# Weight checks read as 16-bit halves, padding rows copied by DMA, and relative keys transposed on TensorE, in a two-layer attention and feed-forward kernel

## The chip, the cores and the metric

One NeuronCore of a Trainium2 chip runs the whole program in one launch. The metric is the device time of one execution in microseconds (us), the median of several. Times within the kernel count from the start of the profiled span.

## What is computed

The input is x, float32, 4 batches of 1024 tokens of 128 features. There are two halves, each "layernorm, layer, layernorm, add to x". The first layer is causal attention with 16 heads of 8 features and relative keys, the second a gated feed-forward network with ternary weights (-1, 0, 1) and a scale per output.

```python
scores = jnp.einsum('bhid,bhjd->bhij', q, k)
rel = jnp.einsum('bhid,pd->bhip', q, rel_key)          # 256 relative keys
rel_idx = jnp.clip(j - i + p - 1, 0, p - 1)
bias = jnp.take_along_axis(rel, rel_idx, axis=3)
logits = jnp.where(causal, (scores + bias) * scale, -jnp.inf)
attn = jax.nn.softmax(logits, axis=-1)
x = x + _layernorm(attn @ v @ Wo + bo)                 # heads joined
h = silu(xn @ w1.T * s1) * (xn @ w2.T * s2)            # xn = layernorm(x)
h = gelu(h @ h1.T * sh1); h = gelu(h @ h2.T * sh2)
x = x + _layernorm(h @ w3.T * s3)
```

The kernel works on the weights of the feed-forward network in a rounded form, and checks first that this loses nothing: the weights as loaded must have no low bits. The result of this check is one of two flags; a later stage takes another way if a flag is set. With ternary weights it isn't.

## The kernel before, in words

The program has a first stage (lines 319 to 713), a stage that is skipped unless a flag is set (`largest_scores`, line 1291), the attention proper (lines 881 to 1290, here "stage two"), and the feed-forward network (`stage3`, line 1423). Each is a block in which the engines run their own lists of instructions, tied by semaphores, and a block begins when all engines have left the one before. The change lies in the first alone.

Stage one goes through the four batches b. VectorE makes the layernorm of the tokens (`layernorm`, lines 444 to 470: `stats`, `mv`, `var_e`, then `std` from ScalarE's `root`, line 570, then eight instructions that write `xh`). TensorE transposes `xh` (line 663), ScalarE copies the result to `xT` (line 579), TensorE projects q, k and v (lines 673 and 681) into the PSUM tensors `p_q`, `p_k`, `p_v`. ScalarE adds the biases (`qf`, `kf`, lines 609 and 611), and ScalarE and VectorE split q and k into three bfloat16 parts each (`q_parts`, `k_parts`). GpSimd writes a copy of q in another order, `q_turned` (line 435). From k's largest and smallest value (`k_ext`, line 495) and q TensorE computes a bound on each row's scores in `p_tr` (lines 691 to 693), the "shift"; ScalarE and VectorE split it into three parts too (`m_neg`, `m_rest`, `m_parts`, lines 633, 638, 480, 584 and 484), the last two of them one batch later (`shift_rest`, `shift_mid`, `shift_low`). Batch b + 1's layernorm and projections are issued in batch b, ahead of its own bound. For the second and third of its four batches the body is a loop of the sequencers.

SyncE issues every DMA of the stage, in one order: tokens of batch 0 into `x_all` (line 324); eight parameter loads, all counted by one semaphore `s_par` (line 333), the last two being `bv_b` (one row of 512 B written eight times into each of 128 partitions) and `rel_t`, the 256 relative keys of 8 features with features as rows, so that each element of 4 B is a piece of its own; tokens of batch 1; the relative keys' parts to DRAM and back (lines 338 to 345, from `rel_p` and `gx`, which VectorE computes in lines 535 to 546); tokens of batches 2 and 3, each when the ones before have landed; the feed-forward weights into `every`, 5632 columns in 128 partitions (line 353). Then per batch the shift of the batch before (line 359) and nine stores of the parts of q, k and turned q (lines 376 to 382), each when it is made. In the last batch the loads for stage two go ahead of these (lines 369 to 372), when all stores of batch 2 have landed.

TensorE, VectorE and ScalarE each wait for all eight parameters, `s_par` at 8 * 16, before the first projection, before the work on the relative keys, and before the first `qf`. VectorE then also waits for `g_ext`, which comes back from DRAM, before its batch 0 (line 547).

The tensors `q_sb` and `k_sb` of stage two have 96 rows. Loads fill 75 and 72 of them; the rest must be 0 in `q_sb` and 1 in `k_sb`. GpSimd writes them at the start by memsets of rows 64 to 95, 4096 columns each (lines 424 and 425).

The check of the weights has three parts. For each, ScalarE writes `every` rounded to `low_part` (`rounded`, line 591), GpSimd subtracts it (`remainder`, line 404), and ScalarE takes the absolute value with the sum along the row (`largest`, line 596). Parts 0 and 1 are rounded at the end of batch 0; the rest of ScalarE's work stands at the head of the last batch and after it. VectorE joins the sums (lines 553 and 555) before `shift_rest(B - 1)`, line 556.

Of the kernel before, what the change touches and what calls it, by code (L numbers as in the profile page):

```python
# [24 lines left out]
P = 256  # L25
# [123 lines left out]
def build(nc, ctx, x, Wq, bq, Wk, bk, Wv, bv, Wo, bo, rel, w1, s1, w2, s2, h1, sh1, h2, sh2, w3, s3, out):  # L149
# [59 lines left out]
    rel_t = sb("rel_t", [HD, P], F32, one)  # L209
# [27 lines left out]
    low_part = [sb(f"low_part{i}", [128, (HC * E * 2 + HC * HID * 2 + HID) // CHECKS + 1], F32R, one) for i in range(2)]  # L237
# [6 lines left out]
    s_par = sem("s_par")  # L244
    s_gs = sem("s_gs")
# [30 lines left out]
    s_whi, s_wlo, s_wabs, s_wany, s_wsum = (sem(n) for n in ("s_whi", "s_wlo", "s_wabs", "s_wany", "s_wsum"))  # L276
# [42 lines left out]
    with nc.Block() as block:  # L319
        @block.sync  # L320
        def _(sp):
# [5 lines left out]
            for dst, src in ((wq_sb[:, :], Wq), (wk_sb[:, :], Wk), (wv_sb[:, :], Wv),  # L327
                             (bq_c[:, :], bq.rearrange("(p a) -> p a", a=1)),
                             (bk_c[:, :], bk.rearrange("(p a) -> p a", a=1)),
                             (r0_c[:, :], ap(rel.tensor, 0, [[0, H], [1, HD], [1, 1]])),  # L330
                             (bv_b[:, :, :], ap(bv.tensor, 0, [[0, 128], [0, NB], [1, 128]])),
                             (rel_t[:, :], ap(rel.tensor, 0, [[1, HD], [HD, P]]))):
                sp.dma_start(dst, src).then_inc(s_par, 16)
# [13 lines left out]
            for b in range(2, B):  # L347
                sp.wait_ge(s_xin, b * 16)
                tokens(b)
            sp.wait_ge(s_rw, 32)  # L350
# [10 lines left out]
            def batch(b, first, last):  # L361
                if last:

                    sp.wait_ge(s_pool, 16)
                    sp.wait_ge(s_qst, 16 * PARTS * b)
                    sp.wait_ge(s_kst, 16 * PARTS * b)
                    sp.wait_ge(s_mst, 16 * (b - 1))
                    sp.wait_ge(s_rst, 16 * PARTS * b)
                    sp.dma_start(q_rows[:, :], ap(qr_dram, 0, [[DROW, PARTS * HD], [0, PARTS], [1, UH * S]])).then_inc(t_qr[0], 16)
                    load_k(0, 0)  # L370
                    load_q(0, 0)
# [19 lines left out]
        def checked(i):  # L391

            n = every.shape[1] // CHECKS + 1
            c = slice(i * n, min((i + 1) * n, every.shape[1]))
            return every[:, c], low_part[i % 2][:, 0:c.stop - c.start]

        @block.gpsimd
        def _(pool):

            def remainder(i):  # L400

                pool.wait_ge(s_whi, i + 1)
                got, part = checked(i)
                nc.gpsimd.tensor_tensor(part, got, part.bitcast(F32), ALU.subtract).then_inc(s_wlo, 1)
# [17 lines left out]

            for p in range(2):
                step(nc.gpsimd.memset(q_sb[p][64:KROWS, :], 0.0), 9 + 4 * p)
                step(nc.gpsimd.memset(k_sb[p][64:KROWS, :], 1.0), 10 + 4 * p)
                pad = v_sb[p][:, :, :].rearrange("p n (h d) -> p n h d", h=HG)
                step(nc.gpsimd.memset(pad[:, :, :, HD:32], 0.0), 11 + 4 * p)
                step(nc.gpsimd.memset(pad[:, :, :, HD:HD + 1], 1.0), 12 + 4 * p)

            for b in range(B):  # L430
# [6 lines left out]
                if b == 0:  # L437
                    remainder(0)
                    remainder(1)
            remainder(2)  # L440

        @block.vector
        def _(dve):
# [42 lines left out]
            def batch(b, first, last_batch):  # L486
# [10 lines left out]
                dve.wait_ge(s_kx, b * KX + 2)  # L497
                nc.vector.tensor_tensor(k_ext[:, :], k_ext[:, :], g_ext[:, 0:2], ALU.add).then_inc(s_kx, 1)
# [33 lines left out]
            dve.wait_ge(s_par, 8 * 16)  # L532
            nc.vector.tensor_tensor(kb_c[:, :], bk_c[:, :], r0_c[:, :], ALU.add).then_inc(s_gs, 1)

            nc.vector.tensor_scalar(rel_s[:, :], rel_t[:, :], rel_t[:, 0:1], None, ALU.subtract).then_inc(s_gs, 1)
# [11 lines left out]
            dve.wait_ge(s_gld, 16)  # L547
# [21 lines left out]
        def _(act):  # L569
# [16 lines left out]
            def rounded(i):  # L586
                act.wait_ge(s_every, 16 * len(WEIGHTS))
                if i >= 2:
                    act.wait_ge(s_wabs, i - 1)
                got, part = checked(i)  # L590
                nc.scalar.activation(part, got, ACT.Copy).then_inc(s_whi, 1)

            def largest(i):
                act.wait_ge(s_wlo, i + 1)
                _, part = checked(i)
                nc.scalar.activation(part, part.bitcast(F32), ACT.Abs, accum_out=low_max[:, i:i + 1]).then_inc(s_wabs, 1)

            def batch(b, first, last_batch):
                if last_batch:
                    largest(0)  # L600
                    rounded(2)
                    largest(1)
                if not last_batch:
# [7 lines left out]
                nc.scalar.activation(kf[:, :], p_k[:, :], ACT.Identity, bias=kb_c[:, 0:1]).then_inc(s_kf, 1)  # L611
                if not last_batch:
# [26 lines left out]
                if first:  # L639
                    rounded(0)  # L640
                    rounded(1)
# [3 lines left out]
            act.wait_ge(s_par, 8 * 16)  # L645
            act.wait_ge(s_gs, 1)
            batches(act, batch)
            largest(2)
# [3 lines left out]
        def _(pe):  # L652
# [49 lines left out]

            transposes(0, True)
            pe.wait_ge(s_par, 8 * 16)
            project_qk(0, True)
            project_v(0, True)
            pe.wait_ge(s_gs, 10)
# [1204 lines left out]
```

## Time and profile before

| | |
|---|---|
| median of 3 runs | 788.54 us (788.49 to 788.73) |
| profiled execution | 789.45 us, span 787.7 us |
| TensorE busy | 646.7 us, 82% of the span |
| VectorE, ScalarE busy | 565.0 us (72%), 562.4 us (71%) |
| GpSimd busy | 301.0 us (38%) |
| DMA | 52.79 MB in 41169 packets, mean 67 GB/s |
| largest line of the chain that ended last | TensorE, lines 1653 and 1656 (`stage3`), 7% each |

Engine times are sums of spans in which the engine had an instruction in work. In the timeline a row gives start, length, engine, line, operation, output and inputs, the number of instructions merged, and in brackets the idle time before it and what ended that. "SPq" is SyncE issuing a DMA; its length is the time of issue, not of the transfer, and a wait inside merged issues is in it. In the rows by windows, DMA share is the mean busy share of 16 DMA engines and PEclk the TensorE clock that was granted, 1.00 being 2.4 GHz and 0.50 being 1.2 GHz.

### The profile page before, as it was taken

The numbers are of one execution on the slowest core, as the hardware profiler recorded it, in microseconds if no ns is written. First come the engines' busy times: TensorE is split into PE (matmuls) and PEld (weight loads), VectorE is DVE, ScalarE is ACT, GpSimd is POOL, SyncE is SP. The second block draws the span as 40 slices with busy tenths as digits, with TensorE's granted clock in tenths as the row PEclk, the third lists the DMA queues.
The fourth block names the chain that finished last, engine by engine and source line by source line (L and its number), as shares of the span: only waits on it lengthen the run. The fifth ranks groups of instructions, "written<-read, shape, count | busy, mean of one in ns | idle before, by whom it ended". The sixth has DMA issues, their size and how long they took to land. (4 is left out here: it accounts for less than half of the span.)

```text
span 787.7 us, 19097 instructions
## 1 busy us (share of the span) xinstructions
PE 646.7 (82%) x8064; PEld 470.4 (60%) x8064; DVE 565.0 (72%) x927; ACT 562.4 (71%) x657; POOL 301.0 (38%) x190
## 2 busy tenths in 40 slices
PE   0667632679999999999999999987779899898993
PEld 0323310556767667676676766855568678687682
DVE  7589963367877778777787777876665757768546
ACT  0264572369898898988988879887757867778563
POOL 9074233813608136081360722701053181451801
PEclk9986866579999999999999999998989999999998
DMA  3470375311422314223152231514020000000001
GB/s 64 103 247 8 117 200 177 70 31 37 121 62 63 94 36 122 62 64 94 32 125 62 64 93 32 125 30 135 14 81 2 0 1 1 0 28 1 0 28 55
DMA packets 41169, 52.79 MB, mean 67 GB/s; under 512 B 7410, under 2 KB 31554, under 8 KB 38658
## 3 DMA queue, kind: packets, MB, share of 16 engines
q1 hardware_dynamic: 41082, 51.54, 24.3%
q8 instruction: 65, 1.06, 0.6%
q14 instruction: 22, 0.18, 0.1%
HBM read 39.59 MB, written 11.94 MB: 65 GB/s over the span
## 5 line engine op out<-in xcount | busy, mean ns | idle before, releaser
L960 PE MATMUL p_s<-q_sb,k_sb 96*128 96x128 bf16 (+1 forms) x1600 | 170.8, 249 | 18.7 <-DVE probs L1106 14.9
L1224 ACT ACTIVATE probs<-p_s 128x1024 f32<-128x1024 f32 x160 | 156.8, 1018 | 17.8 <-DVE p_s L1115 10.8
L1224 ACT ACTIVATE probs<-probs 128x1024 f32<-128x1024 f32 x128 | 133.7, 1057 | 46.4 <-DVE probs L1106 46.2
L1004 PE MATMUL p_o<-probs,v_sb 128*32 128x128 f32 (+1 forms) x3200 | 159.1, 330 | 7.6 <-ACT o_acc L1242 5.3
L960 PEld LDWEIGHTS p_s<-q_sb,k_sb 96*128 96x128 bf16 x1600 | 112.7, 100 | 77.7 <-issue 29.0
L916 POOL TENSOR_SCALAR_AFFINE_SELECT even_b<-even_b 128x2048 f32<-128x2048 f32 x32 | 75.5, 2360 | 216.3 <-ACT even_b L1235 216.3
L1106 DVE TENSOR_TENSOR probs<-p_s,even_b 128x1024 f32<-128x1024 f32 x96 | 115.0, 1220 | 28.4 <-PE p_s L960 16.0
L1004 PEld LDWEIGHTS p_o<-probs,v_sb 128*32 128x32 f32 x3200 | 84.5, 111 | 40.7 <-issue 13.5
L1653 PE MATMUL p_z<-hid_hi,h_hi 128*128 128x512 f32 x256 | 102.3, 399 | 1.7 <-POOL hid_lo L1574 1.7
L1656 PE MATMUL p_z<-hid_lo,h_hi 128*128 128x512 f32 x256 | 100.8, 394 | 0.0
L981 PE MATMUL p_s<-q_rows,rel_w 72*128 72x64 bf16 x2048 | 84.8, 197 | 18.2 <-DVE probs L1106 8.7
L981 PEld LDWEIGHTS p_s<-q_rows,rel_w 72*128 72x128 bf16 x2048 | 76.9, 101 | 28.1 <-DVE probs L1106 10.7
L1858 DVE TENSOR_TENSOR hid_lo<-act_f,hid_hi 128x512 fp32r<-128x512 f32 x64 | 55.6, 882 | 41.7 <-ACT hid_hi L1756 41.7
L920 POOL TENSOR_SCALAR_AFFINE_SELECT even_b<-even_b 128x2048 f32<-128x2048 f32 x32 | 75.5, 2359 | 7.5 <-POOL even_b L916 7.5
L1127 DVE COPY even_b<-p_s 128x1024 f32<-128x1024 f32 x40 | 48.8, 1221 | 27.7 <-PE p_s L981 27.5
L1755 ACT ACTIVATE act_f<-p_z,sh_c 128x512 f32<-128x512 f32 x64 | 44.4, 694 | 28.5 <-PE p_z L1656 28.4
L1653 PEld LDWEIGHTS p_z<-hid_hi,h_hi 128*128 128x128 f32 x256 | 48.2, 188 | 13.8 <-POOL hid_lo L1574 2.6
L1656 PEld LDWEIGHTS p_z<-hid_lo,h_hi 128*128 128x128 f32 x256 | 48.2, 188 | 10.6
L435 POOL COPY q_turned<-q_parts 128x1024 bf16<-128x1024 bf16 x12 | 30.9, 2581 | 61.8 <-ACT q_parts L620 43.4
L1127 DVE COPY odd_b<-p_s 128x896 f32<-128x896 f32 x32 | 34.8, 1087 | 23.7 <-PE p_s L981 23.7
L1106 DVE TENSOR_TENSOR probs<-p_s,odd_b 128x1024 f32<-128x1024 f32 x32 | 39.1, 1223 | 13.9 <-PE p_s L960 13.9
L1756 ACT ACTIVATE hid_hi<-p_z,sh_c 128x512 fp32r<-128x512 f32 x64 | 44.1, 689 | 0.0
(176 smaller groups left out, 925.0 us busy)
## 6 DMA issues: line engine op xcount, KB each, us to landing
k_sb<-k_dram SPq DMA_DIRECT2D x48, 192.0 KB
q_sb<-q_dram SPq DMA_DIRECT2D x16, 576.0 KB
q_rows<-qr_dram SPq DMA_DIRECT2D x42, 192.0 KB
q_dram<-q_parts SPq DMA_DIRECT2D x12, 256.0 KB, 3.5
k_dram<-k_parts SPq DMA_DIRECT2D x12, 256.0 KB, 3.8
qr_dram<-q_turned SPq DMA_DIRECT2D x12, 256.0 KB, 3.5
x_all<-in_L_attn_x_dram SPq DMA_DIRECT2D x4, 512.0 KB, 4.1
every<-in_L_ffn_h_w_dram SPq DMA_DIRECT2D x2, 1024.0 KB, 8.3
```

The source lines that it names most:

```text
L916: nc.gpsimd.affine_select(out=far, in_=near, compare_op=ALU.is_ge, fill=0.0, base=-1 - r, pattern=[[0, QB], [-1, MCH * RCH]], channel_mult ...
L920: nc.gpsimd.affine_select(out=near, in_=near, compare_op=ALU.is_ge, fill=MASKED, base=r, pattern=[[0, QB], [1, MCH * RCH]], channel_multip ...
L960: last = nc.tensor.matmul(slot[:, c:c + n * BLK], k_sb[hg][:, h * S + j * BLK:h * S + (j + 1) * BLK], ap(q_sb[hg], at, [[HG * S, KROWS], [ ...
L981: last = nc.tensor.matmul(slot[:, x * QB:(x + 1) * QB], rel_w[0:ROWS, w0:w0 + BLK], q[:, r, :, :], start=True, stop=True)
L1004: last = nc.tensor.matmul(p_o[32 * h:32 * h + 32, at:at + blocks * BLK], v_sb[hg][:, j, h * 32:(h + 1) * 32], probs[n % PBUFS][:, h, col * ...
L1106: last = nc.vector.tensor_tensor(probs[m % PBUFS][:, hp * 2:hp * 2 + 2, :], columns(slot, 0, run), term, ALU.add)
L1127: nc.vector.tensor_copy(to, got).then_inc(t_cd, 1)
L1224: nc.scalar.activation(to, got, ACT.Exp, scale=SCALE).then_inc(t_exp, 1)
L1653: nc.tensor.matmul(to[:, :], whi[w][:, j, cols], hi[j], start=(j == 0), stop=False)
L1656: last = nc.tensor.matmul(to[:, :], whi[w][:, j, cols], lo[j], start=False, stop=(j == len(hi) - 1))
L1755: nc.scalar.activation(act_f[k][:, o, :], bank(tile)[:, :], ACT.Gelu, scale=sc).then_inc(f_act, 1)
L1858: nc.vector.tensor_tensor(hid_lo[k][l % 2][:, o, :], act_f[k][:, o, :], hid_hi[k][l % 2][:, o, :].bitcast(F32), ALU.subtract).then_inc(f_l ...
```

## The change

The check of the weights becomes three ScalarE passes, of 2048, 2048 and 1536 columns, at the end of batch 0. Each reads the lower 16 bits of every float as an unsigned number, every other 16-bit number of `every`, and sums them along the row. Nothing of it is left in the last batch, and GpSimd has no part in it. The rows of padding come from a small tile `pads` (two memsets of 512 columns) by four DMAs, issued behind the tokens of batch 3 and waited for on SyncE before `every` is loaded. The relative keys are loaded as they lie, 128 keys in as many partitions, 32 B a piece, first of the parameters, and transposed by two TensorE instructions into `p_v`. VectorE reads them there, with one column copied to `gx` first. The semaphore of the parameters is split: `s_relt` for the keys, `s_wts` for the three weights, `s_par` for the last four. `kb_c` moves behind the work on the relative keys, the wait for `g_ext` moves into batch 0, and in batch 0 ScalarE's `root(1)` moves behind `kf`.

```diff
-    rel_t = sb("rel_t", [HD, P], F32, one)
+    rel_n = sb("rel_n", [128, P // 128, HD], F32, one)
+    pads = sb("pads", [128, 2, 512], BF16, one)
...
-    low_part = [sb(f"low_part{i}", [128, (HC * E * 2 + HC * HID * 2 + HID) // CHECKS + 1], F32R, one) for i in range(2)]
+    low_part = sb("low_part", [128, HC * HID], F32, one)
...
             tokens(0)
-            for dst, src in ((wq_sb[:, :], Wq), (wk_sb[:, :], Wk), (wv_sb[:, :], Wv),
-                             (bq_c[:, :], bq.rearrange("(p a) -> p a", a=1)),
+            sp.dma_start(rel_n[:, :, :], ap(rel.tensor, 0, [[HD, 128], [128 * HD, P // 128], [1, HD]])).then_inc(s_relt, 16)
+            for dst, src in ((wq_sb[:, :], Wq), (wk_sb[:, :], Wk), (wv_sb[:, :], Wv)):
+                sp.dma_start(dst, src).then_inc(s_wts, 16)
+            for dst, src in ((bq_c[:, :], bq.rearrange("(p a) -> p a", a=1)),
...
-                             (bv_b[:, :, :], ap(bv.tensor, 0, [[0, 128], [0, NB], [1, 128]])),
-                             (rel_t[:, :], ap(rel.tensor, 0, [[1, HD], [HD, P]]))):
+                             (bv_b[:, :, :], ap(bv.tensor, 0, [[0, 128], [0, NB], [1, 128]]))):
                 sp.dma_start(dst, src).then_inc(s_par, 16)
...
             for b in range(2, B):
                 sp.wait_ge(s_xin, b * 16)
                 tokens(b)
+            sp.wait_ge(s_pool, 9)
+            for p in range(2):
+                for rows, dst, which in ((ROWS + PARTS, q_sb[p], 0), (ROWS, k_sb[p], 1)):
+                    n = KROWS - rows
+                    sp.dma_start(ap(dst, rows * (HG * S), [[HG * S, n], [512, HG * S // 512], [1, 512]]),
+                                 ap(pads, which * 512, [[2 * 512, n], [0, HG * S // 512], [1, 512]])).then_inc(s_pads, 16)
+            sp.wait_ge(s_pads, 16 * 4)
             sp.wait_ge(s_rw, 32)
...
                 if last:
-                    sp.wait_ge(s_pool, 16)
...
+            nc.gpsimd.memset(pads[:, 0, :], 0.0)
+            step(nc.gpsimd.memset(pads[:, 1, :], 1.0), 9)
             for p in range(2):
-                step(nc.gpsimd.memset(q_sb[p][64:KROWS, :], 0.0), 9 + 4 * p)
-                step(nc.gpsimd.memset(k_sb[p][64:KROWS, :], 1.0), 10 + 4 * p)
...
-                if b == 0:
-                    remainder(0)
-                    remainder(1)
-            remainder(2)
...
+                if first:
+                    dve.wait_ge(s_gld, 16)
                 nc.vector.tensor_tensor(k_ext[:, :], k_ext[:, :], g_ext[:, 0:2], ALU.add).then_inc(s_kx, 1)
...
             layernorm(0, True)
-            dve.wait_ge(s_par, 8 * 16)
-            nc.vector.tensor_tensor(kb_c[:, :], bk_c[:, :], r0_c[:, :], ALU.add).then_inc(s_gs, 1)
-            nc.vector.tensor_scalar(rel_s[:, :], rel_t[:, :], rel_t[:, 0:1], None, ALU.subtract).then_inc(s_gs, 1)
+            rel_t = p_v[0:HD, 0:P]
+            dve.wait_ge(s_gtr, 1)
+            nc.vector.tensor_copy(gx[:, 2:3], rel_t[:, 0:1]).then_inc(s_gs, 1)
+            dve.wait_ge(s_gs, 1)
+            nc.vector.tensor_scalar(rel_s[:, :], rel_t, gx[:, 2:3], None, ALU.subtract).then_inc(s_gs, 1)
...
-            dve.wait_ge(s_gld, 16)
+            dve.wait_ge(s_par, 4 * 16)
+            nc.vector.tensor_tensor(kb_c[:, :], bk_c[:, :], r0_c[:, :], ALU.add).then_inc(s_gs, 1)
...
-            def rounded(i):
+            def low_bits(i):
                 act.wait_ge(s_every, 16 * len(WEIGHTS))
-                if i >= 2:
-                    act.wait_ge(s_wabs, i - 1)
-                got, part = checked(i)
-                nc.scalar.activation(part, got, ACT.Copy).then_inc(s_whi, 1)
-            def largest(i):
-                act.wait_ge(s_wlo, i + 1)
-                _, part = checked(i)
-                nc.scalar.activation(part, part.bitcast(F32), ACT.Abs, accum_out=low_max[:, i:i + 1]).then_inc(s_wabs, 1)
+                if i > 0:
+                    act.wait_ge(s_wabs, i)
+                n = every.shape[1]
+                c = slice(i * (HC * HID), min((i + 1) * (HC * HID), n))
+                low = every[:, c].bitcast(mybir.dt.uint16).rearrange("p (c two) -> p c two", two=2)[:, :, 0]
+                nc.scalar.activation(low_part[:, 0:c.stop - c.start], low, ACT.Copy,
+                                     accum_out=low_max[:, i:i + 1]).then_inc(s_wabs, 1)
             def batch(b, first, last_batch):
-                if last_batch:
-                    largest(0)
-                    rounded(2)
-                    largest(1)
-                if not last_batch:
+                if not first and not last_batch:
                     root(b + 1)
...
                 nc.scalar.activation(kf[:, :], p_k[:, :], ACT.Identity, bias=kb_c[:, 0:1]).then_inc(s_kf, 1)
+                if first:
+                    root(1)
...
                 if first:
-                    rounded(0)
-                    rounded(1)
+                    for i in range(CHECKS):
+                        low_bits(i)
             root(0)
             transposed(0, True)
-            act.wait_ge(s_par, 8 * 16)
-            act.wait_ge(s_gs, 1)
+            act.wait_ge(s_par, 4 * 16)
+            act.wait_ge(s_gs, 10)
             batches(act, batch)
-            largest(2)
             shift_mid(B - 1)
...
+            pe.wait_ge(s_relt, 16)
+            for x in range(P // 128):
+                last = nc.tensor.transpose(p_v[0:HD, x * 128:(x + 1) * 128], rel_n[:, x, :], ident[:, :])
+            last.then_inc(s_gtr, 1)
             transposes(0, True)
-            pe.wait_ge(s_par, 8 * 16)
+            pe.wait_ge(s_wts, 3 * 16)
             project_qk(0, True)
+            pe.wait_ge(s_gs, 2)
             project_v(0, True)
-            pe.wait_ge(s_gs, 10)
+            pe.wait_ge(s_gs, 11)
             batches(pe, batch)
```

## Rows read from the trace of the kernel before

**Rows 1.** Windows, stage one: busy time (instructions) by engine, PEclk, DMA share, GB/s

```profile
0.00:137.30 137.30, 64.50 (x180) 30.33 (x180) 100.32 (x183) 57.89 (x66) 60.49 (x35) 0.81 0.47 131
```

**Rows 2.** Timeline, 11 to 19 us, VectorE and GpSimd: start, length, engine, line

```profile
11.09 8.65 DVE L468 TENSOR_SCALAR xh<-x_all,rstd,nmr 128x128 f32<-128x128 f32 x8
...
14.99 3.54 POOL L425 MEMSET k_sb<- 32x4096 bf16 x1
```

**Rows 3.** DMA packets of 8 to 18 and of 18 to 22 us, tokens' issue and landing

```profile
DMA packets 882, 0.39 MB, mean 39 GB/s; under 512 B 116, under 2 KB 882, under 8 KB 882
...
DMA packets 2364, 0.22 MB, mean 54 GB/s; under 512 B 1956, under 2 KB 2364, under 8 KB 2364
...
5.74 14.11 SPq L323 DMA_DIRECT2D x_all<-in_L_attn_x_dram  x1
...
DMA to landing us min/median/max: 4.1/4.1/19.9
```

**Rows 4.** SyncE's issues 26 to 39 us, landing of the weights, window 38 to 48 us

```profile
26.96 0.31 SPq L338 DMA_DIRECT2D g_dram<-rel_p  x1
...
30.82 4.51 SPq L323 DMA_DIRECT2D x_all<-in_L_attn_x_dram  x2
35.37 1.44 SPq L353 DMA_DIRECT2D every<-in_L_ffn_w_w_dram  x2
...
38.15 0.78 SPq L353 DMA_DIRECT2D every<-in_L_ffn_w_w_dram  x1
...
DMA to landing us min/median/max: 4.3/7.4/9.7
...
38.00:48.00 10.00, 9.31 (x20) 3.94 (x19) 9.90 (x12) 6.09 (x7) 7.04 (x2) 0.69 1.04 354
```

**Rows 5.** Timeline, 24 to 38 us, VectorE and ScalarE

```profile
24.28 0.16 DVE L533 TENSOR_TENSOR kb_c<-bk_c,r_c 128x1 f32<-128x1 f32 x1 [4.54 <-DMA rel_t<-in_L_attn_rel_key_dram]
...
31.52 1.64 DVE L449 BATCH_NORM_STATS2 stats<-x_all 128x6 f32<-128x128 f32 x8
...
34.27 0.21 ACT L572 ACTIVATE std<-var_e 128x8 f32<-128x8 f32 x1 [11.80 <-DVE var_e L456]
...
34.96 2.23 DVE L468 TENSOR_SCALAR xh<-x_all,rstd,nmr 128x128 f32<-128x128 f32 x8
...
37.10 1.22 DVE L495 TENSOR_REDUCE k_ext<-kf 128x1 f32<-128x1024 f32 x1
```

**Rows 6.** Timeline, 52 to 64 us, ScalarE, GpSimd and VectorE

```profile
52.61 3.41 ACT L591 ACTIVATE low_part<-every 128x1878 fp32r<-128x1878 f32 x2
54.45 7.61 POOL L404 TENSOR_TENSOR low_part<-every,low_part 128x1878 fp32r<-128x1878 f32 x2 [3.08 <-ACT low_part L591]
55.92 0.19 ACT L572 ACTIVATE std<-var_e 128x8 f32<-128x8 f32 x1
...
58.75 5.18 DVE L468 TENSOR_SCALAR xh<-x_all,rstd,nmr 128x128 f32 x8
```

**Rows 7.** Timeline, 101 to 110 us, ScalarE at the head of the last batch

```profile
101.24 1.76 ACT L596 ACTIVATE low_part<-low_part 128x1878 fp32r<-128x1878 f32 x1
...
108.60 1.05 ACT L620 ACTIVATE q_parts<-qf 128x1024 bf16<-128x1024 f32 x1
```

**Rows 8.** Window 110 to 124 us, landing of the shifts, the end of stage one

```profile
110.00:124.00 14.00, 8.09 (x12) 2.22 (x12) 12.20 (x13) 5.77 (x7) 7.58 (x4) 0.67 0.78 189
...
DMA to landing us min/median/max: 2.2/2.3/6.1
...
125.02 1.06 ACT L638 ACTIVATE m_parts<-m_neg 16x1024 bf16<-16x1024 f32 x1 [2.65 <-DMA m_dram<-m_parts]
127.03 1.77 ACT L596 ACTIVATE low_part<-low_part 128x1876 fp32r<-128x1876 f32 x1 [0.95 <-POOL low_part L404]
...
129.20 1.20 DVE L480 TENSOR_TENSOR m_rest<-m_neg,m_parts 16x1024 f32<-16x1024 f32 x1
```

**Rows 9.** Window 160 to 168 us, where TensorE's work of stage two comes back

```profile
160.00:168.00 8.00, 6.26 (x72) 4.41 (x72) 5.95 (x6) 5.06 (x5) 1.11 (x3) 0.56 0.07 20
```

More of the change, by code:

```diff
@@ L244, in build @@
     s_par = sem("s_par")
+    s_wts = sem("s_wts")
+    s_relt = sem("s_relt")
+    s_pads = sem("s_pads")
+    s_gtr = sem("s_gtr")
     s_gs = sem("s_gs")
@@ L275, in build @@
     s_every = sem("s_every")
-    s_whi, s_wlo, s_wabs, s_wany, s_wsum = (sem(n) for n in ("s_whi", "s_wlo", "s_wabs", "s_wany", "s_wsum"))
+    s_wabs, s_wany = sem("s_wabs"), sem("s_wany")
     s_qst, s_kst, s_mst = sem("s_qst"), sem("s_kst"), sem("s_mst")
@@ L389, in _ @@
             sp.wait_ge(s_mst, 16 * B)
[L391 to L395, printed above, removed]
         @block.gpsimd
         def _(pool):
-            def remainder(i):
-                pool.wait_ge(s_whi, i + 1)
-                got, part = checked(i)
-                nc.gpsimd.tensor_tensor(part, got, part.bitcast(F32), ALU.subtract).then_inc(s_wlo, 1)
             def step(ins, n):
@@ L421, in _ @@
             step(nc.gpsimd.memset(gap_one[:, :], 0.0), 8)
+            nc.gpsimd.memset(pads[:, 0, :], 0.0)
+            step(nc.gpsimd.memset(pads[:, 1, :], 1.0), 9)
             for p in range(2):
-                step(nc.gpsimd.memset(q_sb[p][64:KROWS, :], 0.0), 9 + 4 * p)
-                step(nc.gpsimd.memset(k_sb[p][64:KROWS, :], 1.0), 10 + 4 * p)
                 pad = v_sb[p][:, :, :].rearrange("p n (h d) -> p n h d", h=HG)
-                step(nc.gpsimd.memset(pad[:, :, :, HD:32], 0.0), 11 + 4 * p)
-                step(nc.gpsimd.memset(pad[:, :, :, HD:HD + 1], 1.0), 12 + 4 * p)
+                step(nc.gpsimd.memset(pad[:, :, :, HD:32], 0.0), 10 + 2 * p)
+                step(nc.gpsimd.memset(pad[:, :, :, HD:HD + 1], 1.0), 11 + 2 * p)
             for b in range(B):
@@ L584, in shift_mid @@
                 nc.scalar.activation(m_parts[:, 1, :], m_rest[:, :], ACT.Identity).then_inc(s_mhi, 1)
-            def rounded(i):
+            def low_bits(i):
                 act.wait_ge(s_every, 16 * len(WEIGHTS))
-                if i >= 2:
-                    act.wait_ge(s_wabs, i - 1)
-                got, part = checked(i)
-                nc.scalar.activation(part, got, ACT.Copy).then_inc(s_whi, 1)
-            def largest(i):
-                act.wait_ge(s_wlo, i + 1)
-                _, part = checked(i)
-                nc.scalar.activation(part, part.bitcast(F32), ACT.Abs, accum_out=low_max[:, i:i + 1]).then_inc(s_wabs, 1)
-            def batch(b, first, last_batch):
-                if last_batch:
-                    largest(0)
-                    rounded(2)
-                    largest(1)
-                if not last_batch:
+                if i > 0:
[5 more added lines that the diff above has]
+                                     accum_out=low_max[:, i:i + 1]).then_inc(s_wabs, 1)
+            def batch(b, first, last_batch):
+                if not first and not last_batch:
                     root(b + 1)
```

## The prediction, made before the changed kernel ran

> **What bounds the kernel now.** I read the page first (which engine is busy where), then the windows by stage, then the timeline of the first 137 us with the SyncE queue's own waits, and last the landing times of single tiles. Everything the diff touches lies in stage one. It takes 137.3 us, and no engine fills it: VectorE, the busiest, has 100.3 us, and DMA a share of 0.47 [rows 1]. A chain through several engines bounds it, so each removed piece must be followed to what waits for it next. For the end of the run only one moment counts, the end of stage one: what follows starts from it as before.
>
> At the start, GpSimd's memsets of 32x4096 hold VectorE's normalisation: the eight xh instructions spread over 8.65 us beside memsets of 3.5 us [rows 2], and need 2.23 us with GpSimd idle [rows 5]. But TensorE, VectorE (kb_c) and ScalarE then wait for the parameters until 24.28 us [rows 5], so this is hidden. Of the parameters two are slow. bv_b reads one row of 512 B 1024 times: between 8 and 18 us 882 packets moved only 0.39 MB, 39 GB/s. Only after it come the 2048 four-byte pieces of rel_t: 1956 small packets between 18 and 22 us. The second batch's tokens, issued at 5.74, stand behind both and land after 19.9 us, at 25.7 [rows 3]. The change removes rel_t alone.
>
> **The start of the change.** The relative keys come as 256 pieces of 32 B instead, transposed by two TensorE instructions and read from PSUM; 256 pieces at the small packets' rate of rows 3 (1956 in under 4 us) are 0.5 us, the added copy of one column some 0.15 us, and both finish before xh. Without long memsets xh ends near 10.6; transposes and the q, k projections start by 13.4 instead of 24.3. bv_b stays: its 524 KB at 39 GB/s [rows 3] are 13.4 us, from about 6 to 19.5, and the tokens behind it (512 KB, at the 354 GB/s of rows 4 1.5 us, and near 0.5 to land) arrive near 21.5. That, not the projections, is what VectorE waits for: the second layernorm starts at 21.5 instead of 31.52. With root(1) moved behind kf nothing is late (kf is through by 22, the root is due at 24.2). So k_ext comes at 27.2 instead of 37.10 [rows 5]: **9.9 us earlier**.
>
> **The SyncE queue.** It is here that the change adds a wait. Its stores of the relative keys stand behind the same tokens and land near 21.6; from the store at 26.96 to the third tokens at 30.82 lay 3.9 us, of which about 1.6 were the stores themselves, so 2.3 remain and those tokens go out near 24.0; the fourth need them landed (4.1 us, rows 3) and go at 28.2. Now four new DMAs are issued, 0.6 us each, to about 31, of 21, 24, 21 and 24 rows by 8 KB, 737 KB in all, and the queue waits for them to land, with the five loads of `every` and all stores of batch 0 behind it. Their rate is unknown. The nearest rows are the loads into 72 and 24 rows of the same tiles, 189 GB/s [rows 8]: 3.9 us. The fast end is the 354 GB/s of whole loads [rows 4], 2.1 us; the slow end the 39 GB/s of the other source that is read over and over [rows 3], 19 us. I take 3.9: after the tokens' data at 31.8 the pads land near 36.0. `every` is then first issued at 36.05, where it was 35.37. Before, it ran behind the fourth tokens; the last was issued at 38.15 and landed 9.7 us later, at 47.9. Behind an idle queue 2.88 MB at 354 GB/s are 8.1 us, with the 2.2 that a small transfer takes from issue to landing [rows 8]: **46.4**.
>
> A rule speaks against these DMAs. The Trainium skill, DMA: Bandwidth & Descriptors, section on why a DMA increments its semaphore by 16, says that a transfer uses the largest number of engines up to 16 that divides the slowest dimension of both sides. By it the 21-row transfers run on 7 engines and the 24-row ones on 12. No run here shows the pads yet; the share of 0.78 (12.5 of 16 engines) of rows 8 for 24-row loads agrees. By it the first seven engines carry 80 packets of 1 KB each, with which my 3.9 us would be 49 ns a packet, so the sum would not move much.
>
> **ScalarE.** The two rounding passes of batch 0 started at 52.61, moved to 42.7, and the weights are there at 46.4 to 46.5: 3.8 us of new waiting. Three passes of 2048, 2048 and 1536 columns follow. From 1.05 us for 1024 and 1.76 for 1878 an element costs 0.83 ns [rows 7]: 1.90, 1.90 and 1.48, with 0.18 for the accumulator each, 5.8 to 5.9 in all; two rounding passes cost 3.3 (to the root at 55.92). That the input is every other 16-bit number is not shown: the low end is the same rate, the high end twice it, 4.7 us more; I take the same, since cost per element there went with the count. So the root comes at 52.4 and xh ends 2.9 us behind it (34.27 to 37.19, rows 5), at 55.4. Before, GpSimd's subtractions (from 54.45, 7.6 us) held VectorE: xh began at 58.75 and ended at 63.93 [rows 6]. **8.5 us earlier**, of which 9.9 came in, 3.8 went to the weights, 2.6 to the longer passes, and 5.0 came from GpSimd no longer working beside xh.
>
> **The end of stage one.** Batches 1 and 2 keep their length. In batch 3 the three ScalarE passes from 101.24 are gone, so VectorE's part runs 3 to 5 us sooner (q_parts, at 108.60, only 1, as its buffer waits for batch 2's stores). I count this as hidden: the last m_parts pass, at 125.02, waited 2.65 us for the shift of batch 2, whose store took 6.1 us instead of 2.3, because it stands behind the loads for stage two, which run at a share of 0.78 between 110 and 124 us [rows 8] and start no earlier than before. Behind it largest(2) goes: the final subtraction could begin at 126.1 instead of 129.20: **3.1 us** [rows 8]. GpSimd's last subtraction was beside all this. Were the shift not held, the other stores, moved by the same DMA, would still cap the tail at about 4.6.
>
> Sum: 8.5 + 3.1 = 11.6 us. The profiled execution took 789.45 us (span 787.7), 0.9 over the median of 788.54; 777.9 against it, **776.9** against the median.
>
> **Rivals.**
> 1. The weights come in time, because the pads or bv_b are quicker than thought. Then the passes start at 42.7, the gain at xh is 12.3, with the tail 15.4: 773.1; with the capped tail another 1.5 less, 771.6. For it: nothing has been seen of pads; against: the wait for them is plain, and bv_b's rate is shown. 0.17.
> 2. The strided 16-bit read costs double (gain 6.9, 781.6), or the pads pay bv_b's 13 ns (766 large packets in 10 us, rows 3) for each of 720 packets, 9.4 instead of 3.9 us (gain 6.1, 782.4). For: both forms are new. 0.13.
> 3. **Slower**: the pads go at bv_b's 39 GB/s, since each source row is read 8 times. They take 19 us instead of 3.9, SyncE holds `every` and batch 0's stores 15 us longer, and ScalarE stands before root(2): 15 - 11.6 = 3.4 slower, 792. It turns slower once the pads take over 15.5 us, 48 GB/s. Against: bv_b's rows all came from one place in HBM, these are 90 rows in SBUF. 0.04.
> 4. The start-up gain doesn't show because the tokens, not the layernorm's helpers, were all that mattered: bv_b lasts 4 us longer than I take, with rel_n's pieces among it: gain 7.6, 781. 0.06.
> 5. The clock: TensorE has 0.56 of it between 160 and 168 us when its work comes back [rows 9]. How that falls against work that comes 12 us sooner is open: a few microseconds more or less at half rate, partly hidden behind VectorE; I put 2 us either way on it, within the range.
>
> **The numbers.** My forecast has 0.60, the rivals 0.17, 0.13, 0.04 and 0.06. The range takes in rivals 1, 2 and 4 with the unknown rates: 771.0 to 783.0. Under 0.2% (1.6 us) a measurement of this kernel tells little from no change. Faster 0.93, same 0.03 (pads near 14 us), slower 0.04.
>
> **What the profile after would show.** xh of batch 0 near 8.5 to 10.6, at 2.2 us; stats of the second batch at 21 to 22, behind its tokens; the third tokens at 24, four pad issues at 28 to 31, `every` first issued near 36 (if at 33, rival 1; if beyond 45, rival 3); low_bits behind a wait on `every` at about 46.5, 1.9 us a pass; xh of batch 2 unstretched, ending at 55.4; 3.1 us less between the last m_parts pass and the end of stage one. I am wrong if low_bits starts without a wait, if a pass takes over 2.5 us, if batches 1 and 2 change their length, or if the stages behind differ by more than 2 us.

## The result, and the profile after

The changed kernel takes 783.01 us (781.41 to 783.46, 4 runs) where the kernel before took 788.63 (788.49 to 789.47): ratio 0.9924, interval 0.9910 to 0.9938, so 4.9 to 7.1 us less. The profiled execution took 783.46 us (span 781.7) against 789.45. The forecast was 776.9 in a range of 771.0 to 783.0: the median lies on the upper edge, on the side that was forecast, with half of the gain.

The first 32 us of the changed kernel's timeline, VectorE (start, length, engine, line, operation; in brackets the idle time and what ended it):

```profile
8.38 2.14 DVE L464 TENSOR_SCALAR xh<-x_all,rstd,nmr 128x128 f32<-128x128 f32 x8
...
20.20 0.16 DVE L547 TENSOR_TENSOR kb_c<-bk_c,r_c 128x1 f32<-128x1 f32 x1 [6.88 <-DMA bv_b<-in_L_attn_bv_dram]
...
22.27 1.64 DVE L445 BATCH_NORM_STATS2 stats<-x_all 128x6 f32<-128x128 f32 x8 [1.82 <-DMA x_all<-in_L_attn_x_dram]
...
27.76 1.22 DVE L491 TENSOR_REDUCE k_ext<-kf 128x1 f32<-128x1024 f32 x1
```

Without the long memsets xh takes 2.14 us instead of 8.65 [rows 2]. The wait for `bv_b` ends at 20.20, the second batch's tokens are there at 22.27 (31.52 before) and k_ext comes at 27.76 instead of 37.10 [rows 5]: 9.3 us earlier, where 9.9 were forecast. In the six other runs that keep this start it comes at 28.37 to 28.82, 8.3 to 8.7 us earlier than in the kernel before.

The timeline of SyncE's queue in the same kernel:

```profile
23.95 4.40 SPq L328 DMA_DIRECT2D x_all<-in_L_attn_x_dram  x2
28.40 0.91 SPq L360 DMA_DIRECT2D q_sb<-pads  x1
...
31.05 0.81 SPq L360 DMA_DIRECT2D k_sb<-pads  x1
...
39.36 0.92 SPq L366 DMA_DIRECT2D every<-in_L_ffn_w_w_dram  x2
...
41.43 0.50 SPq L366 DMA_DIRECT2D every<-in_L_ffn_w_w_dram  x1
```

Its windows around the pads, as a whole and in two parts, and around `every` (window, its length, busy time and instructions of PE, PEld, DVE, ACT, POOL, then PEclk, DMA share and GB/s):

```profile
32.00:39.00 7.00, 7.00 (x14) 2.31 (x13) 7.00 (x5) 3.64 (x5) 3.93 (x2) 0.84 0.54 84
...
32.00:34.00 2.00, 2.00 (x3) 0.67 (x2) 2.00 (x2) 1.37 (x2) 1.95 (x1) 0.50 0.76 82
...
36.00:38.00 2.00, 2.00 (x6) 0.74 (x6) 2.00 (x3) 1.19 (x2) 1.81 (x1) 1.00 0.45 105
...
42.00:50.00 8.00, 1.36 (x13) 1.17 (x11) 2.03 (x10) 1.06 (x2) 0.21 (x1) 0.87 0.95 319
```

And the time from issue to landing of `every`'s DMAs in the same kernel, shortest, median and longest:

```profile
DMA to landing us min/median/max: 2.8/7.4/10.2
```

The third tokens go out at 23.95 and the pads at 28.40, as forecast to 0.2 us. Then comes the gap: from 31.9, when the last pad DMA has been issued, SyncE issues nothing for 7.5 us. The pads move at 84 GB/s over a share of 0.54, and `every` goes out at 39.36, 4.0 us later than before the change (35.37, rows 4), in spite of the earlier start. The last of its pieces, issued at 41.43, takes the longest of these times, 10.2 us, to land.

The timeline of ScalarE and VectorE where batch 0 ends, in the same kernel:

```profile
51.69 1.91 ACT L594 ACTIVATE low_part<-every 128x2048 f32<-128x2048 uint16 x1 [8.59 <-DMA every<-in_L_ffn_w_w_dram]
53.50 0.19 ACT L594 ACTIVATION_READ_ACCUMULATOR low_part<-every 128x1 f32 x1
...
57.35 0.19 ACT L572 ACTIVATE std<-var_e 128x8 f32<-128x8 f32 x1
...
58.12 2.14 DVE L464 TENSOR_SCALAR xh<-x_all,rstd,nmr 128x128 f32 x8
```

ScalarE stands 8.59 us for the weights. The passes then take 1.91 us for 2048 columns, 1.90 being what the other ScalarE rows give for as many: reading every other 16-bit number cost nothing more here. The root of batch 2 comes at 57.35, later than the 55.92 of before [rows 6]. What is gained here is all behind it: xh is no longer stretched by GpSimd and ends at 60.26 instead of 63.93, 3.7 us sooner.

The timeline of the last batch and the end of stage one, in the same kernel; the PE row is the first of stage two:

```profile
103.96 1.06 ACT L617 ACTIVATE q_parts<-qf 128x1024 bf16<-128x1024 f32 x1 [4.44 <-DMA k_dram<-k_parts]
...
121.24 1.06 ACT L635 ACTIVATE m_parts<-m_neg 16x1024 bf16<-16x1024 f32 x1 [5.42 <-DMA m_dram<-m_parts]
122.33 1.21 DVE L476 TENSOR_TENSOR m_rest<-m_neg,m_parts 16x1024 f32<-16x1024 f32 x1 [5.49 <-ACT m_parts L635]
...
125.90 0.35 SPq L372 DMA_DIRECT2D m_dram<-m_parts  x1
...
130.52 1.71 PE L982 MATMUL p_s<-q_rows,rel_w 72*128 72x64 bf16 x29 [5.50 <-PEq L1325]
```

The same first row of stage two in the kernel before:

```profile
137.37 1.86 PE L981 MATMUL p_s<-q_rows,rel_w 72*128 72x64 bf16 x32 [5.49 <-PEq L1324]
```

The three passes at the head of the batch are gone, but q_parts waits 4.44 us for the stores of batch 2 and the m_parts pass 5.42 us, not 2.65 [rows 8], for the shift's store. From that pass to m_rest it is 1.1 us instead of 4.2: 3.1 us. Stage two starts 6.85 us earlier (3.7 and 3.1). From there to the end of the execution this profile takes 652.9 us and the one before 652.1, which leaves 6.0.

### The profile page after: what moved, and what is told of

The parts are those of the page before. It is cut to its first block and busy times, and to the rows that moved or that the text cites. A ratio compares the mean times of both kernels' runs of the same rounds, so it can differ in the third digit from the quotient of the medians.

```text
span 781.7 us, 19102 instructions
## 1 busy us (share of the span) xinstructions
PE 648.1 (83%) x8066; PEld 471.8 (60%) x8066; DVE 551.1 (70%) x928; ACT 557.1 (71%) x654; POOL 273.9 (35%) x185
## 3 DMA queue, kind: packets, MB, share of 16 engines
q1 hardware_dynamic: 40056, 52.28, 24.6%
## 5 line engine op out<-in xcount | busy, mean ns | idle before, releaser
L1225 ACT ACTIVATE probs<-probs 128x1024 f32<-128x1024 f32 x128 | 133.5, 1055 | 46.4 <-DVE probs L1107 46.2
L435 POOL COPY q_turned<-q_parts 128x1024 bf16<-128x1024 bf16 x12 | 28.9, 2407 | 81.0 <-ACT q_parts L617 62.6
```

Source lines behind the costliest of these rows:

```text
L1225: nc.scalar.activation(to, got, ACT.Exp, scale=SCALE).then_inc(t_exp, 1)
```

## The experiments

Two theories stood against each other. Q: the check brings the gain, while the earlier start is eaten on SyncE's queue, where `every` stands behind the pads, and these behind tokens that stand behind `bv_b`. S: the earlier start itself carries at least half. Medians are compared with the change's 783.0 and with the kernel before, timed beside each group of them (789.1, 789.1 and 789.5).

### Each half of the change alone

**a1_check_alone**: the kernel before, with the new check and nothing else of the change (the edit in short).

```diff
-    rounded(0), rounded(1) at the end of batch 0; largest(0), rounded(2), largest(1), largest(2) later
-    remainder(0..2) on GpSimd
+    for i in range(CHECKS):
+        low_bits(i)                 # end of batch 0
```

> The kernel before with the new check alone: three low_bits passes at the end of batch 0, GpSimd's subtractions and the passes of the last batch gone; parameters, relative keys and memsets as before. Theory Q (the gain sits in the check; the start of the change is eaten by the wait for the weights on SyncE's queue): the weights are there at 47.9, the passes run from 52.6 to 58.5 without a wait, xh of batch 2 ends at 61.4 instead of 63.93 (2.5 us), and 3.1 us more come at the end of stage one: about 783.0, as fast as the whole change. Rival S (the earlier start carries at least half of the change's 5.6 us): at most 3 us of gain, 785.6 or more.

Measured: 784.04 us, ratio 0.9919 (0.9889 to 0.9950). The timeline of this kernel, ScalarE, VectorE and the first row of stage two:

```profile
53.59 1.89 ACT L578 ACTIVATE low_part<-every 128x2048 f32<-128x2048 uint16 x1
...
60.00 2.14 DVE L452 TENSOR_SCALAR xh<-x_all,rstd,nmr 128x128 f32 x8
...
132.62 6.58 PE L959 MATMUL p_s<-q_rows,rel_w 72*128 72x64 bf16 x119 [5.49 <-PEq L1302]
```

The passes start without a wait, 1 us later than forecast: half of that because this execution's parameters came 0.5 us later, the other half inside batch 0. xh ends at 62.1.

**a2_start_alone**: the changed kernel, with the check of before put back (in short).

```diff
-    low_bits(0..2)
+    rounded, remainder and largest as before
```

> The changed kernel with the check of before: rounding on ScalarE, subtraction on GpSimd, three passes in the last batch. Theory Q: the rounding starts when the weights land, 51.7 instead of 52.6, GpSimd then holds xh of batch 2 as before, and the rest of stage one is as before: about 1 us of gain, 787.6. Rival S: 3 us or more of gain, 785.6 or less.

Measured: 789.05 us, ratio 0.9994 (0.9983 to 1.0006). The timeline of this kernel, ScalarE, GpSimd and VectorE:

```profile
52.67 3.43 ACT L607 ACTIVATE low_part<-every 128x1878 fp32r<-128x1878 f32 x2 [9.36 <-DMA every<-in_L_ffn_w_w_dram]
54.52 7.62 POOL L416 TENSOR_TENSOR low_part<-every,low_part 128x1878 fp32r<-128x1878 f32 x2 [11.71 <-ACT low_part L607]
58.84 5.18 DVE L480 TENSOR_SCALAR xh<-x_all,rstd,nmr 128x128 f32 x8
```

Here some 9 us of earlier start come to nothing, where 1 us was expected: ScalarE waits 9.36 us for the weights and rounds at 52.67, where the kernel before did at 52.61 [rows 6]; xh is stretched to 5.18 us as before. The check alone gives what the whole change gives, within the intervals. S falls. The traces leave the start a smaller part beside the new check: stage two begins 4.75 us earlier in a1 (132.62) and 6.85 in the change, so 2.1 us between two single executions, of which at least 0.5 are a1's late parameters.

### What holds the weights

**a3_pads_behind**: the pads behind `every`, their wait ahead of the loads for stage two.

```diff
-    pads: four DMAs; sp.wait_ge(s_pads, 16 * 4)
     every: five DMAs
+    pads: four DMAs
...
                 if last:
+                    sp.wait_ge(s_pads, 16 * 4)
```

> The changed kernel with the four pad DMAs issued behind the loads of every, and their landing waited for only ahead of the loads for stage two. Theory Q: every is issued at 28.4 instead of 39.4 and has landed by 42, the passes start when ScalarE comes to them at 43.1 instead of 51.7, and the run is 8.6 us shorter: 774.4. Rival D (the transfers themselves bound this stretch, in whatever order they go): every still lands after 47, and the gain is under 4 us.

Measured: 774.95 us (0.9809, 0.9785 to 0.9833). The timeline of this kernel, SyncE's queue and ScalarE:

```profile
29.21 1.13 SPq L359 DMA_DIRECT2D every<-in_L_ffn_w_w_dram  x2
...
44.73 1.89 ACT L594 ACTIVATE low_part<-every 128x2048 f32<-128x2048 uint16 x1
```

The row of the pass has no wait: the weights are there when ScalarE comes, 1.6 us later than forecast, of which 0.6 had come up by k_ext. One place in the queue is worth 8 us. Against a1, which has the new check and the old start (784.04), it is 9.1 us: with the pads out of the way nearly all of the earlier start arrives.

**b2_no_wait**: the pads where they are; only the wait moves.

```diff
     pads: four DMAs
-    sp.wait_ge(s_pads, 16 * 4)
```

> The changed kernel with the pad DMAs where they are, but their landing waited for only ahead of the loads for stage two, so the loads of every are issued right behind them at 31.9. It parts the cost of the wait on SyncE from that of the transfer. If the slow pads hold their DMA engines until 39 as well (queues in order), every lands near 47.5 and the gain is about 4 us (779); if every flows past them, it lands by 44 and the gain is 7 us or more (776 or less).

Measured: 779.28 us (0.9864, 0.9840 to 0.9889). The timeline of this kernel, SyncE's queue and ScalarE:

```profile
33.80 2.34 SPq L365 DMA_DIRECT2D every<-in_L_ffn_w_w_dram  x2
36.19 3.57 SPq L365 DMA_DIRECT2D every<-in_L_ffn_h_w_dram  x2
39.80 2.73 SPq L365 DMA_DIRECT2D every<-in_L_ffn_w_w_dram  x1
...
50.38 1.91 ACT L594 ACTIVATE low_part<-every 128x2048 f32<-128x2048 uint16 x1 [6.19 <-DMA every<-in_L_ffn_w_w_dram]
```

The five issues of `every` now last 8.7 us instead of 2.6, with the pads still on their way; that SyncE can't hand its pieces over meanwhile is the likely reason, and no run shows it by itself. The profiled execution was the slowest of four (783.52 us), so its trace is a poor measure of the gain. In the trace the passes come 1.3 us sooner, in an execution whose root of batch 1 was 1.0 us late (25.98 instead of 24.94); the median is 3.7 us lower. Of the 8.1 us that a3 gives back the wait alone is thus 1.3 to 3.7, the lesser part, and the rest is the transfer; the two numbers don't fix the split closer.

**b3_pads_32_rows**: why the transfer is slow.

```diff
-                for rows, dst, which in ((ROWS + PARTS, q_sb[p], 0), (ROWS, k_sb[p], 1)):
+                for rows, dst, which in ((64, q_sb[p], 0), (64, k_sb[p], 1)):
```

> The changed kernel with the four pad DMAs filling rows 64 to 95 in each tile (32 rows instead of 21 and 24; the extra rows are overwritten by later loads), 1.05 MB instead of 0.74. It asks what makes the pads slow, 8.7 us of transfer. If it is the number of DMA engines that the row count allows (7 and 12, with 80 packets on the first seven), 32 rows go over 16 engines with 64 packets each at the same time per packet and take 7 us: every lands 1.7 us earlier, 781.5. If it is the few rows at one side of the memory (24 rows took 85 GB/s), 32 rows take 9.3 us: 0.6 us or more later, 783.5 to 784.5.

Measured: 782.08 us (0.9898, 0.9876 to 0.9921). The window of this kernel's pads, columns as above:

```profile
32.00:37.00 5.00, 5.00 (x7) 1.92 (x6) 5.00 (x4) 3.22 (x5) 2.47 (x2) 0.54 1.10 201
```

And the timeline of its SyncE queue, the issue behind them:

```profile
38.34 0.93 SPq L366 DMA_DIRECT2D every<-in_L_ffn_w_w_dram  x2
```

With 42% more bytes the transfer is faster: 201 GB/s at a full share, against 84 at 0.54, and `every` goes out 1.0 us sooner, in an execution whose root of batch 1 was 0.7 late. The share times 16 engines times the window, divided by the packets of 1 KB that the rate makes in it, gives 0.105 us a packet in the change and 0.090 here: on the average a packet costs nearly the same, and the number of engines makes the difference. By the Trainium skill, DMA: Bandwidth & Descriptors, section on why a DMA increments its semaphore by 16, 21 rows go over 7 engines, 24 over 12, 32 over 16. The traces agree: in the change the share is 0.76 (12.2 of 16 engines) between 32 and 34 us and 0.45 (7.2 of 16) between 36 and 38, when by the same count the 24-row transfers are through; here it is full. A limit by the rows alone doesn't fit, as 32 rows are at most half more than 21 and the rate is 2.4 times as high.

The average hides something. By the same division a packet of the change took 0.15 us between 32 and 34 us and 0.07 between 36 and 38: twelve engines moved 82 GB/s where seven moved 105 later. What slowed the first stretch was not tried. The medians of this run and of the change differ by less than their intervals; the verdict rests on the windows.

### What holds the start

**a4_bv_once**: `bv_b` as one row in each partition, 128 pieces instead of 1024, repeated in VectorE's reading.

```diff
-                             (bv_b[:, :, :], ap(bv.tensor, 0, [[0, 128], [0, NB], [1, 128]]))):
+                             (bv_b[:, :], ap(bv.tensor, 0, [[0, 128], [1, 128]]))):
...
-                                bv_b[:, :, :].rearrange("p n (g x) -> p g n x", g=BG), ALU.add)
+                                bv_b[:, :].rearrange("p (g x) -> p g x", g=BG).unsqueeze(2).broadcast_to([128, BG, NB, 128 // BG]), ALU.add)
```

> The changed kernel with bv loaded as one row of 512 B into each partition (128 pieces instead of 1024) and repeated over the eight blocks by VectorE's access pattern. Theory Q: the tokens of batch 1 land near 9.5 instead of 22.2, the SyncE queue is 6 to 7 us earlier (third tokens at 17 instead of 24), pads landed at 32.5, every at 45, passes from 45: 6.8 us shorter, 776.2. Rival (tokens are held by something other than the repeated row): they land at 22 as before and nothing changes, 783.0.

Measured: 776.60 us (0.9827, 0.9802 to 0.9853). The timeline of this kernel, VectorE, SyncE's queue and ScalarE:

```profile
13.49 1.62 DVE L445 BATCH_NORM_STATS2 stats<-x_all 128x6 f32<-128x128 f32 x8
...
20.67 0.20 DVE L456 RECIPROCAL rstd<-std 128x8 f32<-128x8 f32 x1 [4.56 <-ACT std L572]
...
33.45 0.92 SPq L366 DMA_DIRECT2D every<-in_L_ffn_w_w_dram  x2
...
46.31 1.91 ACT L594 ACTIVATE low_part<-every 128x2048 f32<-128x2048 uint16 x1 [8.84 <-DMA every<-in_L_ffn_w_w_dram]
```

The tokens no longer hold the second layernorm (13.49, no wait), `every` goes out 5.9 us sooner, and the passes still wait 8.84 us for it. The load of `bv_b` had held the whole queue. What holds the second layernorm now is `root(1)`, which the change put behind `kf`: VectorE waits 4.56 us for its `std`. Putting it back ahead was not tried.

**b1_behind_and_bv**: the edits of a3 and a4 together.

> Both edits of a3_pads_behind and a4_bv_once. Theory Q: with bv as one row the tokens of batch 1 are early and batch 0's own work sets its end; in a4 that work ran 4.5 us earlier than in the changed kernel (k_sel at 26.0 instead of 30.5), so ScalarE comes to the passes near 39 and the weights, issued near 22, are there: 5.5 us shorter than a3, about 769.5. Rival: the passes still wait for the weights beyond 43, 773 or more.

Measured: 767.81 us (0.9723, 0.9694 to 0.9753). The timeline of this kernel, ScalarE and the first row of stage two:

```profile
38.65 1.89 ACT L594 ACTIVATE low_part<-every 128x2048 f32<-128x2048 uint16 x1
...
117.34 7.06 PE L982 MATMUL p_s<-q_rows,rel_w 72*128 72x64 bf16 x128 [5.50 <-PEq L1325]
```

The passes start at 38.65 without a wait. Beside a3, where the weights are no longer waited for, the one row of `bv` is worth 7.1 us more (774.95 less 767.81): with the queue in order, a start made earlier reaches the end. In a4, where they are waited for, it was worth 6.4 (783.01 less 776.60), since there it brought the weights forward too.

### The end of the stage

**b4_second_shift**: a second tile for the last batch's shift.

```diff
+    m_last = sb("m_last", [H, PARTS, S], BF16, one)      # in place of m_parts where b == B - 1
...
-                if not first:
+                if not first and not last_batch:
                     act.wait_ge(s_mst, b * 16)
```

> The changed kernel with a second tile for the shift of the last batch, so that its first part need not wait for the store of batch 2's shift. Theory of the prediction: the m_parts pass starts at 115.9 instead of 121.24, but its final store stands behind the other stores, which drain until 126.6 whatever happens, so the stage ends about 1.5 us sooner: 781.5. Rival: only that wait mattered, and the stage ends 5 us sooner, 778.

Measured: 781.77 us (0.9899, 0.9879 to 0.9918). The timeline of this kernel, ScalarE, SyncE's queue and TensorE:

```profile
53.69 1.91 ACT L598 ACTIVATE low_part<-every 128x2048 f32<-128x2048 uint16 x1 [9.82 <-DMA every<-in_L_ffn_w_w_dram]
...
117.22 1.06 ACT L639 ACTIVATE m_last<-m_neg 16x1024 bf16<-16x1024 f32 x1
...
121.89 0.35 SPq L376 DMA_DIRECT2D m_dram<-m_last  x1
...
131.58 7.05 PE L986 MATMUL p_s<-q_rows,rel_w 72*128 72x64 bf16 x128 [10.80 <-PEq L1329]
```

This execution came to the passes 2.0 us late (53.69), so times are taken from there. The last store is issued 68.2 us behind them instead of 74.2 (125.90 less 51.69), but stage two starts 77.9 us behind them instead of 78.8: of 6.0 us, 0.9 arrive. Its own store takes 7.3 us to land instead of 2.2, behind the other stores, as the prediction had it. The median is 1.2 us lower, which the intervals don't tell apart from the change.

**c1_all_second_shift**: b1 and b4 together.

> b1_behind_and_bv with the second shift tile of b4_second_shift. The two gains lie at different places of the path and should add: 1.0 to 1.5 us less than b1, 766.5. If the stores of the last batch are what ends the stage, no more than that.

Measured: 767.48 us (0.9714, 0.9692 to 0.9736), not told apart from b1 by its interval, though stage two started at 115.82 instead of 117.34.

### A version that beats both

**c2_passes_late**: the passes moved to the last batch.

```diff
-                if first:
+                if last_batch:
                     for i in range(CHECKS):
                         low_bits(i)
```

> The changed kernel with the three low_bits passes moved from the end of batch 0 to the last batch, ahead of the m_parts pass, where ScalarE stood 5.4 us waiting for the shift's store. Theory Q: the root of batch 2 no longer waits for the weights and comes 14.2 us earlier, at 43.1. Next in line are then the stores of batch 0, held on SyncE by the same wait for the pads: they land near 54, and q_parts of batch 1, at 63.0 in the changed kernel, can't go before. So 8 us of gain, 775; without such a next wait it would be 14, 769.

Measured: 773.21 us (0.9793, 0.9768 to 0.9817). The timeline of this kernel, ScalarE:

```profile
44.88 0.19 ACT L572 ACTIVATE std<-var_e 128x8 f32<-128x8 f32 x1
...
56.65 1.06 ACT L617 ACTIVATE q_parts<-qf 128x1024 bf16<-128x1024 f32 x1 [6.04 <-DMA k_dram<-k_parts]
...
113.59 1.05 ACT L638 ACTIVATE m_parts<-m_neg 16x1024 bf16<-16x1024 f32 x1 [1.20 <-DMA m_dram<-m_parts]
```

The root of batch 2 comes 12.5 us sooner, and the next wait stands there as expected: 6.04 us on batch 0's stores, which SyncE had held behind the pads. In the last batch the three passes lie inside the wait for the shift's store, of which 1.20 us are left.

**c3_late_and_both**: c2 with the edits of a3 and a4.

> c2_passes_late with the pads behind every and bv as one row. The passes (5.9 us) leave batch 0 and lie where ScalarE waits anyway; the stores of batch 0 are issued 9 us earlier than in c2, so they hold q_parts of batch 1 little. 5 to 5.5 us less than b1_behind_and_bv: 762.5. Rival: the stores hold batch 1 again, and the gain over b1 stays under 2 us.

Measured: 764.90 us (763.38 to 767.05), ratio 0.9676 (0.9651 to 0.9700). The timeline of this kernel, ScalarE and TensorE:

```profile
46.32 1.06 ACT L617 ACTIVATE q_parts<-qf 128x1024 bf16<-128x1024 f32 x1 [1.15 <-DMA k_dram<-k_parts]
...
113.79 7.06 PE L982 MATMUL p_s<-q_rows,rel_w 72*128 72x64 bf16 x128 [5.50 <-PEq L1325]
```

24.6 us less than the kernel before and 18.1 less than the change; 2.9 less than b1 (the two intervals just overlap), short of the 5 to 5.5 expected. Stage two starts 3.5 us sooner than in b1 (113.79, 117.34), not 5.5: q_parts still waits 1.15 us for stores.

## Why the prediction was half right

- **The start.** Right in kind and nearly in size. That `bv_b` and not `rel_t` holds the tokens, and that the tokens and not the projections bound the second layernorm, was read from the packets [rows 3]; k_ext came 9.3 us earlier for 9.9. a4 confirms the cause. But the weights bound what follows, so little of it arrived: the sum gave the start 6.1 us (9.9 less 3.8), and ScalarE began on the weights 0.9 us earlier, at 51.69 instead of 52.61.
- **The new wait on SyncE.** The step that failed is its size: "I take 3.9" for the pads. The sum was made with the rate of the nearest loads, 189 GB/s [rows 8]; the pads made 84. They were through, and `every` was issued, at 39.36 instead of 36.05: 3.3 us. The prediction had the reason in hand, in the sentence on the number of engines, and put it aside because 3.9 us over 80 packets on the first seven engines would be 49 ns a packet. That is a circle: the 49 ns come from the 3.9 us and say nothing of what a packet costs. A packet took some 0.1 us on the average, 80 of them 8 us. Nor does the share of 0.78 in rows 8 bear the rule out, since the window holds loads of 72 and of 24 rows, gaps and stores. The loads of rows 8 move long rows from DRAM, these are pieces of 1 KB within SBUF, and the rate of one was carried to the other; which of the two differences made a packet dear was not tried. Rival 2 came nearest; its source was a repeated row, though, while b3 shows the same repeated rows at 201 GB/s over more engines.
- **The landing of the weights.** A second miss at the same place: 10.4 us were reckoned from the first issue to the landing, at 354 GB/s. It took 12.3. The queue was idle ahead of it, and that bought nothing: before the change it was 12.5 us from the first issue at 35.37 to the landing at 47.9 [rows 4], in a4 12.9. Between 42 and 50 us the rate was 319 GB/s, and the stores of batch 0, issued from 42 us on, share it. So the passes began at 51.69 instead of 46.4 to 46.5, and with 0.2 us saved in them the root was 4.95 late. In b4 they began at 53.69, so about 2 us of this place vary between executions.
- **ScalarE and GpSimd.** Right: 1.91 us a pass for 1.90, xh of batch 2 unstretched at 2.14 us, batches 1 and 2 unchanged (61.0 us from the end of xh to the last batch's m_parts pass, 61.1 before).
- **The tail.** Right: 3.1 us, q_parts gaining only 1 us over the rest, and the larger part of the three removed passes hidden behind the loads' DMAs. b4 shows the cap, 0.9 us more, of 1.5 that the prediction allowed without a working.
- **The rest.** Stage two began 6.85 us earlier for 11.6. The part behind it took 0.9 us longer in the profiled execution, within the 2 us set aside for rival 5. The clock fits: TensorE was busy at the lower clock for about 46 us of that part, and for 41 before (summed over windows of 2 us).

Rivals 1 and 4 did not occur, nor did rival 3: the pads' transfer, some 8 us, stayed under the 15.5 us at which it would have turned the sign. But a2 shows how near the start came to that: without the new check, all of it was lost. That the measured time lies just at the edge of the range, and not outside, is owed to the width given for the unknown rate of the pads.

## What to carry to other kernels

Work on one in-order DMA queue is on the path of everything issued behind it: put what is needed first at its head, and what only a later stage needs behind that, before paying for it with a wait. When a transfer's rate is taken from another, take one with the same piece size, the same source and the same count of rows; the count of rows alone made 84 GB/s into 201 (b3). A saving ahead of a wait is worth nothing unless what is waited for comes sooner too: 9 us of earlier start gave nothing while the weights came no sooner (a2), and some 9 us once they did (a3 against a1); the edit of `bv_b` gave 6.4 us under the same wait, as it brought the weights forward (a4).

## What the runs showed of the hardware

One row of 512 B read 1024 times came at 39 GB/s [rows 3], and held the tokens behind it for 12 us: they landed 16.6 us after their issue in the changed kernel and 4.7 in a4, where it is read 128 times. The tokens are 1024 pieces of 512 B too, from different rows, and reached 352 GB/s in a4, so neither the size of the pieces nor their number was the limit. Transfers within SBUF in pieces of 1 KB ran at 84 GB/s with 21 and 24 rows, and at 201 with 32.

The part behind stage one, which no edit touched, took between 649.5 and 653.9 us in thirteen profiled executions (from the first matmul of stage two to the execution's time), so 4.4 us of difference between two profiled executions can come from there. In it are short stretches at the lower clock, at other places in each kernel. The first two windows are of the changed kernel, the third and fourth of the one before:

```profile
208.00:212.00 4.00, 4.00 (x52) 2.55 (x49) 2.54 (x3) 2.80 (x3) 0.00 (x0) 0.57 0.30 86
259.00:263.00 4.00, 4.00 (x49) 2.48 (x49) 2.71 (x4) 2.95 (x4) 0.00 (x0) 0.57 0.32 93
```

```profile
412.80:416.20 3.40, 3.40 (x32) 2.06 (x24) 2.02 (x3) 2.21 (x3) 0.00 (x0) 0.50 0.32 101
464.00:467.40 3.40, 3.40 (x36) 2.08 (x32) 2.26 (x3) 2.50 (x3) 0.00 (x0) 0.50 0.45 121
```

TensorE was busy all through them, but not ahead: in the 4 us before each of the four it was busy for 2.75 to 2.76. Ahead of the first stands a wait of 1.25 us for `probs` from VectorE, until 207.85. The kernel before has the same wait until 214.76, and there the clock stayed at 1.00, so what else brings the stretches on is open. The time that TensorE was busy at the lower clock goes with the length of this part: 35 us of it in b1 (649.7 us), 41 before (652.1), 46 in the changed kernel (652.9), 49 in b2 (653.9), and a correlation of 0.88 over the thirteen.
